# Decoder layer with cross-attention: turning the normed x1 on VectorE instead of TensorE, and the order of the work around it

## The reference

```python
x = _layernorm(x + self_attention(x, ...))          # x1
q, k, v = split(x @ Wq.T), split(ctx @ Wk.T), split(ctx @ Wv.T)
attn = softmax(where(mask, q @ k.T / sqrt(16), -inf))
x = _layernorm(x + merge(attn @ v) @ Wo.T)           # x2
base = x @ W_base + b_base
h = relu(x @ W_enc[n] + b_enc[n]);  recon = h @ W_dec[n] + b_dec[n]      # n = 0..7
adp = connected_idx[argmin_n mean((recon - x)**2)]   # per sequence
y = base + relu(x @ W_down[adp] + b_down[adp]) @ W_up[adp] + b_up[adp]
out = _layernorm(x + y)
```

## Time and profile before

| what | value |
|---|---|
| three runs | 1650.35, 1651.15, 1655.78 us |
| the profiled execution's own time | 1650.58 us |
| its span, first to last instruction | 1648.8 us |
| busy: TensorE, VectorE, ScalarE, GpSimd | 96%, 75%, 64%, 10% of the span |
| chain that ended last | TensorE 85%, VectorE 7%, ScalarE 3% |
| mean granted TensorE clock | 0.989 of full speed |
| front, eight batches, tail | 0 to 120.93, to 1598, to 1648.8 us |

### The profile page before, as it was taken

How to read it: one execution, slowest core, us unless ns; L and a number is a source line. 1 busy time by engine, 2 the same in 40 slices (tenths; PEclk the granted TensorE clock), 3 DMA queues, 4 the chain that set the end, 5 groups by cost and what they waited for, 6 DMA issues and landing times.

```text
span 1648.8 us, 25559 instructions
## 1 busy us (share of the span) xinstructions
PE 1586.7 (96%) x9632; PEld 588.7 (36%) x9632; DVE 1238.2 (75%) x1790; ACT 1053.2 (64%) x1998; POOL 161.2 (10%) x151
## 2 busy tenths in 40 slices
PE   6779999999999999999999999999999999999997
PEld 5442323332333333332333323433333323332233
DVE  5788777877788777887888777887778777887522
ACT  2227776676666666676666766676666776666661
POOL 7311000100011000100001000110001000000000
PEclk8899999999999999999999999999999999999999
DMA  5655071623517071442707163361707234150010
GB/s 156 116 143 101 25 138 41 101 69 86 96 40 127 28 131 40 90 93 62 116 22 134 32 113 69 69 112 52 121 12 122 61 52 77 50 78 5 11 33 16
DMA packets 118663, 125.22 MB, mean 76 GB/s; under 512 B 35186, under 2 KB 100339, under 8 KB 118540
## 3 DMA queue, kind: packets, MB, share of 16 engines
q1 hardware_dynamic: 117724, 123.06, 38.3%
q10 hardware_dynamic: 816, 0.53, 0.1%
HBM read 84.18 MB, written 35.03 MB: 72 GB/s over the span
## 4 chain that ended last, share of the span: by engine, by line
PE 85%; DVE 7%; ACT 3%; issue 3%; DMA 1%; SPq 0%; POOL 0%; POOLq 0%; DVEq 0%; ACTq 0%
PE banks L1122 23%; PE values L1141 23%; PE banks L1082 12%; PE work L1012 5%; PE work L998 5%; PE work L957 4%; DVE xneg_max_pieces L1439 4%; PE work L1019 3%; PE work L1025 3%; ACT xprobs L1260 3%; PE work L1004 2%; PE work L1028 1%; PE work L942 1%; PE work L1037 1%; DMA max_dram<-xneg_max_rows 1%
## 5 line engine op out<-in xcount | busy, mean ns | idle before, releaser
L1260 ACT ACTIVATE xprobs<-banks 128x512 f32<-128x512 f32 x1664 | 900.5, 595 | 408.3 <-PE banks L1122 405.0
L1439 DVE TENSOR_REDUCE xneg_max_pieces<-banks 128x2 f32<-128x1024 f32 x768 | 909.0, 1219 | 258.4 <-PE banks L1082 257.2
L1122 PE MATMUL banks<-xq_stacks,xk_stacks 99*128 99x512 bf16 (+1 forms) x1664 | 517.7, 385 | 9.9 <-ACT xprobs L1260 3.0
L1141 PE MATMUL values<-xprobs,xv_rows 128*17 128x512 f32 x3328 | 437.9, 598 | 1.3 <-ACT xprobs L1260 1.3
L1122 PEld LDWEIGHTS banks<-xq_stacks,xk_stacks 99*128 99x128 bf16 (+1 forms) x1664 | 127.4, 97 | 398.8 <-ACT xprobs L1260 273.2
L1082 PE MATMUL banks<-xk_stacks,xq_stacks 49*128 49x512 bf16 (+1 forms) x2048 | 250.3, 335 | 14.2 <-DVE xneg_max_pieces L1439 12.3
L1082 PEld LDWEIGHTS banks<-xk_stacks,xq_stacks 49*128 49x128 bf16 x2048 | 57.2, 94 | 327.6 <-DVE xneg_max_pieces L1439 212.9
L1510 POOL TENSOR_TENSOR xk_parts<-xk_rest,xk_parts 128x401 bf16<-128x401 f32 (+1 forms) x64 | 59.0, 923 | 660.5 <-ACT xk_parts L1239 660.5
L1141 PEld LDWEIGHTS values<-xprobs,xv_rows 128*17 128x17 f32 x3328 | 55.1, 95 | 122.9 <-issue 117.6
L1505 POOL TENSOR_TENSOR xrstd<-xrstd,mhalf 128x4 f32<-128x4 f32 x23 | 23.2, 1011 | 652.4 <-DVE xrstd L1314 652.4
L1012 PEld LDWEIGHTS work<-xvT,ctxT_a 128*128 128x128 f32 (+1 forms) x416 | 54.3, 192 | 13.6 <-issue 3.9
(11 more groups left out here) (295 smaller groups left out, 1007.3 us busy)
## 6 DMA issues: line engine op xcount, KB each, us to landing
xk_stacks<-key_parts_dram SPq DMA_DIRECT2D x186, 200.1 KB, 13.0
key_parts_dram<-xk_parts SPq DMA_DIRECT2D x144, 100.0 KB, 2.2
xq_stacks<-parts_dram SPq DMA_DIRECT2D x186, 64.0 KB, 8.8
ctxT_a<-in_ctxT SPq DMA_DIRECT2D x4, 1601.0 KB, 7.5
ctxT_b<-in_ctxT SPq DMA_DIRECT2D x4, 1601.0 KB, 7.5
parts_dram<-xq_parts SPq DMA_DIRECT2D x45, 128.0 KB, 2.0
key_parts_dram<-xk_parts SPq DMA_DIRECT2D x48, 100.2 KB, 5.2
xa<-in_x SPq DMA_DIRECT2D x8, 512.0 KB, 16.3
```

Of the source, the lines that this page charges most:

```text
L1122: pe.matmul(at, kst[0:ROWS[par], k, h2, par, t * P:(t + 1) * P], qst[0:ROWS[par], k, h2, par, :], start=True, stop=True).then_inc(made, 1)
L1141: last = pe.matmul(av[32 * j:32 * j + HD + 1, :], vals[:, k, t, gr * GH + j, :], probs[:, sl % 2, j, :], start=t == 0, stop=t == XKT - 1)
L1260: nc.scalar.activation(probs[:, sl % 2, j, :], score_bank(n)[0], ACT.Exp).then_inc(exped, 1)
L1439: nc.vector.tensor_reduce(nmp[:, of % 2, :, j2, q, piece], pairs[n % MRING][:, :, :], AX.X, ALU.max, negate=True).then_inc(on["mxr"], 1)
```

## The change

1. `x1T` is gone from TensorE and ScalarE. VectorE turns `xa` into `xT` by 16 transposes a batch, each of 32 partitions by 256 values in blocks of 32x32 (step `turn`, slots 13 to 22), and `qproj 0` and the reload of `xa` wait for their semaphore.
2. The table of side jobs is rearranged: `qproj 0` moves from slots 12, 13 to 23, 24; `v 2` to 12, 13; `v 3` gets the end of slot 14; `kproj 4` moves from 22 to 25; `gram 2` has two parts instead of three; `x2T 1` moves from 16 to 15, `loss` from 35 to 34.
3. In slot 5 VectorE does `scale` before `apply`; `invert` 1, `scale` 1 and `choose` move by a slot.
4. The loss product has two rows instead of three; the bias squares are added once at the start.
5. SyncE's list: the query parts come after the maxima of group 2; `key_parts 4` and the load of the context come after the outputs of group 1 instead of before them.
6. The tail's two layer norms go by halves, the adapter's bias has its own semaphore that only ScalarE waits for, and the constant part of the loss is made earlier.

```diff
-            8: ("x1T", 0, NEXT), 11: ("x1T", 1, NEXT), 14: ("x2T", 0, PREV), 16: ("x2T", 1, PREV), 18: ("v", 3, NOW),
-            35: ("loss", 0, PREV),
+        IN_BETWEEN = {14: ("x2T", 0, PREV), 15: ("x2T", 1, PREV), 34: ("loss", 0, PREV)}
...
+            13: turn_steps(0, 1), 14: [("invert", "o", 0, NOW), *turn_steps(1, 2)], 15: turn_steps(2, 3),
+            16: turn_steps(3, 5), 17: turn_steps(5, 7), 18: [("scale", "o", 0, NOW), *turn_steps(7, 8)],
+            19: turn_steps(8, 9), 20: turn_steps(9, 11), 21: turn_steps(11, 14), 22: turn_steps(14, N_TURNS),
...
-            5: [*norm_steps("apply", "x1", 0, 2, NEXT), ("scale", "o", 3, PREV)],
+            5: [("scale", "o", 3, PREV), *norm_steps("apply", "x1", 0, 2, NEXT)],
...
+            elif name == "turn":
+                a, c = divmod(q, P // 32)
+                if q == 0:
+                    v.wait_ge(on["normed"]["x1"], b)
+                v.transpose(xT[32 * c:32 * (c + 1), :, :].rearrange("p k (n a i) -> p a k n i", a=P // 32, i=32)[:, a],
+                            xa[32 * a:32 * (a + 1), :, :].rearrange("p n (k c i) -> p c k n i", k=CH, i=32)[:, c]
+                            ).then_inc(x1_turned, 1)
...
-                    for c in range(CH):
-                        last = v.scalar_tensor_tensor(lrows[:, 1 + c, :], bdec[:, :, c], xsum[:, c:c + 1], bsq[:, c, :],
-                                                      ALU.mult, ALU.add)
-                    last.then_inc(lrows_ready, 1)
+                    dve_link(v.scalar_tensor_tensor(lpart[:], bdec[:, :, 0], xsum[:, 0:1], bsq[:, 0, :], ALU.mult, ALU.add))
+                    v.scalar_tensor_tensor(lrows[:, 1, :], bdec[:, :, 1], xsum[:, 1:2], lpart[:], ALU.mult, ALU.add
+                                           ).then_inc(lrows_ready, 1)
...
             sp_move_outputs(m)
+            sp_spread_inverses(m)
+            sp_max_rows(m + 2)
             if nxt < B:
                 sp_query_parts(0, uses_before(0, nxt))
-            sp_spread_inverses(m)
-            sp_max_rows(m + 2)
+            sp_move_outputs(m + 1)
             if nxt < B:
                 sp_free_key_dram(nxt, 1)
                 sp_key_parts(4, use + 4)
                 if nxt + 1 < B:
                     sp_load_ctx(nxt + 1)
-            sp_move_outputs(m + 1)
-            if nxt < B:
                 sp_stacks(nxt, 0, m + 1)
...
-            pe.wait_ge(t_down_in, 32)
+            pe.wait_ge(t_down_in, 16)
...
+            def by_halves(what):
+                for i in range(2):
+                    added(what, i)
+                    variances(i)
+                for i in range(2):
+                    normed(what, i)
```

More of the change, by code:

```diff
@@ L854, in norm_steps, with turn_steps @@
             return [(step, what, q, rel) for q in range(first, last)]
+        N_TURNS = (P // 32) ** 2
+        def turn_steps(first, last):
+            return [("turn", "x1", n, NEXT) for n in range(first, last)]
         def choose_steps(first, last):
@@ L1001, in pe_job @@
                 if part == 0 and not ph.first:
-                    pe.wait_ge(on["w_free"], ph.order.after(("x1T", 1, b)))
+                    pe.wait_ge(x1_turned, N_TURNS * b)
                 for kin in units(part, parts, CH):
@@ L1030, in pe_job @@
                 pe.wait_ge(lrows_ready, b + 1)
-                for n in range(1 + CH):
-                    last = pe.matmul(W[:, 0:NE], minus2[:], lrows[:, n, :], start=n == 0, stop=n == CH)
+                for n in range(LOSS_ROWS):
+                    last = pe.matmul(W[:, 0:NE], minus2[:], lrows[:, n, :], start=n == 0, stop=n == LOSS_ROWS - 1)
             elif name == "mid":
@@ L1545, in sp_load_x @@
                 nc.sync.wait_ge(on["x1_out"], 16 * (b - 1))
-                nc.sync.wait_ge(on["w_free"], MAIN.order.after(("x1T", 1, b - 1)))
+                nc.sync.wait_ge(x1_turned, N_TURNS * (b - 1))
             nc.sync.dma_start(xa[:], g.x[b].rearrange("(q p) d -> p q d", p=P)).then_inc(on["x_in"], 16)
@@ L2158, in pe_tail @@
             pe.wait_ge(lrows_ready, B)
-            for n in range(1 + CH):
-                one = pe.matmul(tail_loss, minus2[:], lrows[:, n, :], start=n == 0, stop=n == CH)
+            for n in range(LOSS_ROWS):
+                one = pe.matmul(tail_loss, minus2[:], lrows[:, n, :], start=n == 0, stop=n == LOSS_ROWS - 1)
             one.then_inc(t_loss_made, 1)
@@ L2192, in act_tail, with pool_tail, half_norms @@
                              ).then_inc(t_mid_in, 1)
+        def pool_tail(pool):
+            for what in ("x2", "y"):
+                for i in range(2):
+                    of = rstd[:, 1, 2 * i:2 * i + 2]
+                    pool.wait_ge(on["mv_ready"]["x2"], half_norms(what, i))
+                    nc.gpsimd.tensor_tensor(of, of, g.mhalf[:, 0:2], ALU.pow).then_inc(on["rstd_ready"]["x2"], 1)
+        def half_norms(what, i):
+            return 2 * last + (0 if what == "x2" else 2) + i + 1
         def dve_tail(dve):
@@ L2219, in dve_tail @@
             dve.wait_ge(x1_in, 16 * B)
-            for i in range(2):
-                added("x2", i)
-            normed("x2")
+            by_halves("x2")
+            dve.wait_ge(t_x2T_in, CH)
+            dve_link(v.scalar_tensor_tensor(lpart[:], bdec[:, :, 0], xsum[:, 0:1], bsq[:, 0, :], ALU.mult, ALU.add))
+            dve_mark(v.scalar_tensor_tensor(lrows[:, 1, :], bdec[:, :, 1], xsum[:, 1:2], lpart[:], ALU.mult, ALU.add))
             for i in range(NPAIR):
@@ L2228, in dve_tail @@
             v.tensor_tensor(lrows[:, 0, :].rearrange("p (n e) -> p n e", e=2), loss[:].unsqueeze(2).broadcast_to([P, NPAIR, 2]),
-                            halves[:].unsqueeze(1).broadcast_to([P, NPAIR, 2]), ALU.mult)
-            for c in range(CH):
-                one = v.scalar_tensor_tensor(lrows[:, 1 + c, :], bdec[:, :, c], xsum[:, c:c + 1], bsq[:, c, :], ALU.mult, ALU.add)
-            one.then_inc(lrows_ready, 1)
+                            halves[:].unsqueeze(1).broadcast_to([P, NPAIR, 2]), ALU.mult).then_inc(lrows_ready, 1)
             dve.wait_ge(t_loss_made, 1)
@@ L2237, in dve_tail @@
                 dve_choose(step)
-            for i in range(2):
-                added("y", i)
-            normed("y")
+            by_halves("y")
         own_self.close()
@@ L2286, in _ @@
                     pool_batch(b)
-                pool_rstd("x2", last)
-                pool_rstd("y", last)
+                pool_tail(pool)
             @blk.sync
```

49 lines of the change are left out of this document (29 added, 20 removed).

## The result

The changed kernel took 1671.5 us (median of 4 runs, 1668.8 to 1673.0) against 1650.8 of the kernel before (4 runs): ratio 1.0113, 95% interval 1.0093 to 1.0134. It is slower by 1.1%; forecast were 1649.0 us and a range of 1638 to 1657.

What follows compares the result with a forecast made beforehand. TensorE, 96% busy, was taken as the bound. Loop -0.2 and tail -1.9 from 1650.58 gave 1648.5 profiled, 1649.0 as median: "the same", its saving turned into a wait for the maxima; range for 8 in 10, 1638 to 1657.

Steps and rivals of the forecast that it cites:

- Transposes: Slots 8 and 11: transposes leaving TensorE save 0.56 and 0.84, 1.40 us a batch; 1.0 allowed in batch 0.
- Scale: Slot 6, batches 1 to 6: scaling before the applies ends the output projection's stall, all 0.54 us a batch go.
- Nobody reads before the turns: Slot 5: the second part of the applies comes late, but is not read before the turns in slot 13.
- Turns: VectorE, slots 13 to 22: sixteen at 0.43 us, 6.9 us a batch, fit into 10.27 us idle; cost nothing.
- The 2.5 us a batch: VectorE: the skill's 311 ns estimate for eight 128x128 turns, set beside the 6.9 us a batch assumed.
- Table: Rearranged side jobs: slot 26 starts 2.64 us earlier, 0.71 come behind; TensorE's balance -1.93 us in batches 1 to 6.
- Tail: After the loop: norms by halves, smaller loss and the adapter's bias wait gone save 1.9 us together.
- SyncE's list: First key stack 5.0 us later behind the context, delaying slot 39's maxima; batches 1 to 5 net -0.48 us each.
- slots 26 to 38 take 49.2, 2.16 more than before: Batches 1 to 5: slot 39 ready 49.2 us after slot 26 starts, against TensorE's own 47.75.
- Batch 0: It already waits for the maxima, so the whole 5.0 us delay shows: -1.2 + 5.0 + 0.25 = +4.0 us.
- A: Rival at slot 39: queue doesn't hold stacks back or TensorE paces the maxima; saving stands, 1638.4 us; chance 0.40.
- C: Rival on SyncE's queue: key stacks 7.5 us late instead of 5, +15 us, 1664; wait over 3 us; chance 0.09.

Runs made afterwards that it cites:

- the kernel with x late: Changed kernel with only the load of a later x (512 KB) moved on SyncE's queue behind the maxima of group 3: 1649.7 us, ratio 0.9998.

## Why the prediction was wrong

By its steps:

- **Transposes, 1.40 a batch.** Right in place, too small: slots 8 and 11 gained 0.66 + 0.88 = 1.54 in batch 2 of the changed kernel, and the turn by itself is worth 1.7.
- **Scale, 0.54.** Half wrong: slot 6 gained it, slot 7 gave 0.21 back. "Nobody reads before the turns" looked for who waits for the late applies, and not for what is queued behind them on VectorE.
- **Turns.** Right: 435 ns, hidden. The 2.5 us a batch that the prediction set beside this rest on a figure for bf16; sixteen float32 turns over 32 partitions each take 7.0.
- **Table.** TensorE's own balance was -1.36 to -1.56 a batch, not -1.93. Of the 0.37 between, 0.2 are slot 7, 0.2 the moved jobs (they bring 0.48 ahead of slot 26, 0.70 were allowed) and 0.1 the loss (slots 34 and 35 together went from 8.36 to 8.30, 0.06 for 0.15), less 0.14 more from the transposes.
- **Tail, -1.9.** Right, -1.8.
- **SyncE's list: the step that failed.** The forecast had the mechanism and its place right. What failed is the price, "slots 26 to 38 take 49.2, 2.16 more than before": a wait of 1.45 us a batch, and nothing for the slot behind it. The larger part is what it put at nothing without a reason: the slot at half clock, 7.6 us in batches 1 to 5 and 1.5 at slot 39 of batch 0. The smaller is the size of the wait, 12.8 us in batches 1 to 5 against 7.3. About half of these 5.5 is the first key stack, T+16.9 to T+18.0 and 17.4 in the mean where 16.8 were forecast, mostly because the context itself took 8.1 to 8.5 us to land (the page's medians) and not 7.5. The other half is the way from there to the maxima's read, 30.3 in the mean for 29.8.
- **Batch 0, +4.0.** It was +8.1. The first key stack came 6.8 us later than before and not 5.0, the way to the maxima was 0.8 longer, and 1.5 are half clock. The wait in slot 35 was not looked for, but slot 39 waits for the maxima anyway, so what slot 35 waits is missing from the wait at slot 39 and costs nothing on top.

That the forecast came this near with the wait is in part luck. It treated the way from the first key stack to the maxima's read as a fixed 29.8 us, although TensorE makes the maxima in it at its own pace. It held (28.4 to 30.6 in batches 1 to 5 before, 29.6 to 31.1 after) because the transfers set it, with the DMA engines full all the while. Windows of most of this way in batch 2, before and after, with the DMA engines' share in the last column but one:

```profile
593.47:620.50 27.03, 27.03 (x150) 8.87 (x147) 21.09 (x34) 17.47 (x33) 1.17 (x2) 1.00 1.01 139
...
609.00:636.50 27.50, 27.38 (x160) 9.55 (x159) 22.39 (x40) 18.98 (x37) 2.80 (x3) 1.00 1.03 135
```

It is not fixed when the load changes: 25.7 to 27.8 with x moved out of it, 33.6 to 34.6 with the context moved into it.

Against 20.3 us of error in the span (+18.2 for -2.1): 5.5 of waits, 7.6 of clock and 2.0 of TensorE's balance in batches 1 to 5, 4.1 in batch 0, 0.8 in the front, 0.6 in batch 6, less 0.2 at the end. The half clock is about 9 of it in all. The front differs by 117.4 to 122.9 between profiled runs of these kernels, so its 0.8 tells nothing.

Of the rivals, A's reason against the queue was true in so far as the maxima are made at TensorE's pace, on time (T+37.4), and its conclusion false. C came nearest, over 3 us at slot 39 and 1664 us, but by luck: it had the key stacks 7.5 us late, where 4.9 to 6.2 were measured in batches 1 to 5, it had longer waits than were measured, and no half clock behind them. The Trainium skill (DMA: Bandwidth & Descriptors, "Queues, rings and completion order") has each DMA engine start a queue's descriptors in order. The runs agree, in that 512 KB moved from ahead of the maxima's store to behind it brought its landing from 11.2 to 8.3 us in batch 2.

## What to carry to other kernels

Where a large load is put on a queue decides when each small transfer behind it lands, also those issued 30 us later while the engines still carry the backlog: follow the queue from the moved load to every transfer that something waits for. A stretch in which the DMA engines are full moves as a whole with its first transfer, and its length goes with the bytes in it. Loads that nobody needs soon (a next context, a next x, a store of x1) go directly behind the small round trip that TensorE waits for, not ahead of it; then look at the next small transfer behind them, as slot 42 of the kernel with x late shows. And price a wait of TensorE of some 2 to 3 us at up to twice its length.

## What the hardware showed

Late in a wait or behind it the granted clock fell to half for most of a slot, in 12 of 26 cases at slot 39 (all cases of the profiled runs in which slot 38 ended over 0.4 us late). Where it ended up to 1.6 us late (8 cases) the clock never fell, where it ended 2.75 us late or more (7) always. Between them it was mixed: 1.94, 2.15, 2.49, 2.53, 2.58 had it, 1.76, 2.15, 2.29, 2.39 and twice 2.63 had not.

Two shorter waits can do it as well. In the kernel with doubled turns TensorE waited about 1.3 and 1.7 us within slot 23 in each of batches 1 to 6. Its clock stayed at 1.00 in batches 2 and 4 and fell to its lower level in slots 23 and 24 of batches 1, 3, 5 and 6, with the same waits. So the length of the wait alone doesn't decide; what else does stays open.
